# A graph layer on one core: 102 tiles of gathered rows handed from GpSimd's queue to column copies and single-row transfers

## The reference

```python
h = jnp.maximum(_layernorm(x, axis=-1), 0.0)
h_edge = ((h[src] + edge_attr_64) @ W).reshape(-1, H, D)
el = jnp.einsum('ehd,hd->eh', h_edge, attn_l)
er = jnp.einsum('nhd,hd->nh', (h @ W).reshape(-1, H, D), attn_r)
s = el + er[dst]
s = jnp.where(s > 0, s, NEG_SLOPE * s)
ex = jnp.exp(s - jax.ops.segment_max(s, dst, num_segments=N)[dst])
alpha = ex / jax.ops.segment_sum(ex, dst, num_segments=N)[dst]
ft = jax.ops.segment_sum(h_edge * alpha[..., None], dst, num_segments=N)
g = ft.mean(axis=1)
g = (g - g.mean(axis=0)) / jnp.sqrt(g.var(axis=0) + BN_EPS) * bn_gamma + bn_beta
return x + jax.nn.relu(g)
```

## Time and profile before

| | |
|---|---|
| median of 3 runs | 2339.57 us (2338.94 to 2344.23) |
| span of the profiled execution | 2008.4 us |
| the profiled execution's own time | not given in the profile; the median is 331.2 us over the span |
| busy | PE 926.1 us (46%), DVE 1131.0 (56%), ACT 114.1 (6%), POOL 1485.0 (74%) |
| DMA | 157.09 MB, mean 78 GB/s |

### The profile page before, as it was taken

The page is one execution under the profiler, slowest core; times in us unless marked ns, Lnnn a source line. Parts: engine busy times, 40 slices in busy tenths (PEclk is TensorE's granted clock), DMA queues, the critical chain, the costliest instruction groups (busy, mean ns, idle before and its releaser), DMA issues.

```text
span 2008.4 us, 19568 instructions
## 1 busy us (share of the span) xinstructions
PE 926.1 (46%) x6252; PEld 662.6 (33%) x6252; DVE 1131.0 (56%) x3243; ACT 114.1 (6%) x239; POOL 1485.0 (74%) x1579
## 2 busy tenths in 40 slices
PE   3537545434443454344435543544355335534455
PEld 2425333323332332233323322332233223322245
DVE  7878656545554555455545554555455546554565
ACT  3410000000000000000000000000000000000002
POOL 7777777777777777777777777777777777777771
PEclk9758767666776676667766666666666666666676
DMA  8734322322232223222322232223222322232234
GB/s 232 182 70 124 92 59 60 81 70 60 60 85 66 60 60 91 60 59 60 92 60 59 60 92 59 59 60 92 59 60 60 91 60 60 60 91 60 60 69 133
DMA packets 73591, 157.09 MB, mean 78 GB/s; under 512 B 29092, under 2 KB 33712, under 8 KB 66832
## 3 DMA queue, kind: packets, MB, share of 16 engines
q0 software_dynamic: 50208, 53.02, 15.7%
q1 hardware_dynamic: 22162, 99.02, 14.9%
q10 hardware_dynamic: 1112, 3.73, 0.7%
HBM read 144.42 MB, written 9.80 MB: 77 GB/s over the span
## 4 chain that ended last, share of the span: by engine, by line
POOL 67%; issue 22%; DVE 4%; PE 3%; DMA 2%; ACT 0%; ACTq 0%; DVEq 0%; SPq 0%; POOLq 0%
POOL work L696 67%; PE p_s L944 1%; DMA er_run<-er_tab,er_idx 1%; DMA h_tab<-acc 1%; DMA acc<-in_x 1%; PE po L1082 1%; PE pt L933 0%; POOL er_run L710 0%; DVE acc L1261 0%; DVE acc L1259 0%; DVE acc L1569 0%; DVE work L1253 0%; DVE scaled L1251 0%; PE pt L1142 0%; DVE ohT_i L1363 0%
## 5 line engine op out<-in xcount | busy, mean ns | idle before, releaser
L696 POOL DMA_INDIRECT work<-h_tab,srcI x1498 | 1414.0, 944 | 456.5 <-issue 456.2
L1209 DVE COPY elh<-work 128x16 f32<-128x16 f32 x196 | 39.0, 199 | 731.9 <-DMA work<-h_tab,srcI 729.1
L1019 PE MATMUL p_s<-ident,elh 128*32 128x128 f32 x196 | 50.6, 411 | 769.6 <-DVE elh L1209 769.6
L1082 PE MATMUL po<-scaled,work 128*65 128x64 f32 x3104 | 250.0, 257 | 77.8 <-issue 74.8
L1019 PEld LDWEIGHTS p_s<-ident,elh 128*32 128x32 f32 x196 | 25.7, 155 | 780.9 <-DVE elh L1209 777.0
L1082 PEld LDWEIGHTS po<-scaled,work 128*65 128x65 f32 x3104 | 244.6, 173 | 88.1 <-issue 87.2
L982 PE MATMUL p_s<-work,wpair 128*32 128x256 f32 x784 | 235.8, 468 | 15.6 <-DVE p_r L1487 14.0
L969 PE MATMUL pt<-ident,work 128*128 128x128 f32 x784 | 158.2, 353 | 60.6 <-DVE work L1214 59.8
L1569 DVE TENSOR_TENSOR acc<-acc,po 65x64 f32 x776 | 168.3, 217 | 28.8 <-DVE acc L1569 2.7
L969 PEld LDWEIGHTS pt<-ident,work 128*128 128x128 f32 x784 | 124.1, 183 | 89.4 <-DVE work L1214 84.6
L982 PEld LDWEIGHTS p_s<-work,wpair 128*32 128x32 f32 x784 | 100.6, 134 | 146.0 <-issue 68.1
(11 more groups left out here) (212 smaller groups left out, 945.6 us busy)
## 6 DMA issues: line engine op xcount, KB each, us to landing
work<-in_ea_t SPq DMA_DIRECT2D x49, 1024.0 KB, 6.4
ohT_i<-in_dst_n SPq DMA_DIRECT2D x49, 512.0 KB, 3.4
work<-h_tab,srcI POOLq DMA_INDIRECT x1498, 2.5
acc<-hT_tab SPq DMA_DIRECT2D x2, 1562.5 KB, 14.4
h_tab<-acc SPq DMA_DIRECT2D x1, 2887.5 KB
work<-in_x SPq DMA_DIRECT2D x1, 2800.0 KB
out<-work SPq DMA_DIRECT2D x5, 448.0 KB
acc<-in_x ACTq DMA_DIRECT2D x3, 672.0 KB
```

What stands on the lines that cost most here:

```text
L696: pool.indirect_dma_start(out=row, out_offset=None, in_=x if c < RAW else h_tab, in_offset=bass.IndirectOffsetOnAxis(ap=srcI[:, c, j, g:g ...
L1019: m = mm(sT_ps[:, j * P:(j + 1) * P], elh[:, c % 2, j, :, :].rearrange("p h g -> p (h g)"), ident[:, :], start=False, stop=True, skip_grou ...
L1082: m = mm(bank[0:F1, w0:w0 + H * WIN], edge[c % 2][:, j, g, :], scaled[:, j * CG + g, :, :].rearrange("p h w -> p (h w)"), start=(j == 0), ...
```

## The change

Two constants. COL_FIRST goes from NCH = 49 to 5: every chunk from 5 on gets column tiles at group 12, both halves, or only half 0 in chunks with c % 4 = 1 and in the last; that is 11 x 1 + 1 + 32 x 2 = 76 tiles. ROW_FIRST goes from NCH - 1 = 48 to 6: from chunk 6 to 47 five chunks of eight get a row tile at half 1 of group 15, 26 tiles, beside the one of the last chunk. tiles_of leaves these 102 tiles out of POOL's gathers. ScalarE gets 261 batches of 32 column copies and VectorE 43; SP gets 208 batches of 16 single-row transfers more.

```diff
-ROW_FIRST = NCH - 1
+ROW_FIRST = 6
 BATCH = 16
 BATCHES = (3, 2)
 ROW_SPAN, ROW_SHARE = 8, 5
 COL_G = 12
-COL_FIRST = NCH
+COL_FIRST = 5
 COL_BUFS = 4
 COL_BATCH = 32
 COL_BATCHES = (6, 1)
```

## The result

| | median, us | lowest to highest | runs |
|---|---|---|---|
| before | 2340.32 | 2338.94 to 2344.23 | 4 |
| changed | 3053.81 | 3036.99 to 3057.94 | 4 |

The ratio is 1.3032, 95% interval 1.2988 to 1.3075: 713 us slower, where 127 us faster was forecast.

A forecast was written before the change was run, and what follows sets the result against it. POOL's gathers, one every 1.2486 us, were taken to bound the kernel; 102 fewer save 127.4 us, with other engines' added work hidden and 331.2 us outside the span unchanged: 2339.6 - 127.4 = 2212 us, range 2185 to 2295.

The forecast's parts named there:

- the first one: Whole run: profiled span 2008.4 us against median 2339.57; the 331.2 us outside the span are carried unchanged.
- Rival 2: Time outside the span shrinks with the gathers (factor 1.165): saving 148 us, 2191 us; chance 0.12.
- POOL's part: POOL's gathers in the main loop: 102 fewer at 1.2486 us save 127.4 us; a full chunk takes 37.0 us.
- ScalarE's copy: Pitch of ScalarE's column copies with their address instructions: 0.107 us, with ends 0.09 and 0.203.
- ScalarE will come a little late to its exps: Head of ScalarE's chunk: exp's wait for VectorE makes its chunk 37.4 us, covered by 9 us of room.
- SP's part: SP's queue: five batches of 16 row transfers at 6.66 us plus 1.6 for bulk loads, 34.9 us a chunk.
- Hidden, by 2.6 us: Destinations queued behind SP's rows land at 36.7 us; VectorE's make_near asks for them at 39.3.
- rival 4: SP sets the pace: 0.05 us more a row makes 38.9 us a chunk, 2292 us in all; chance 0.07.
- VectorE: VectorE's one column batch a chunk, after the first eight adds: 5.3 us, upper end 8.5, hidden in waits.
- Rival 6: VectorE's copies each stop POOL for 0.14 us, 4.5 us a chunk: 2406 us; chance 0.04.
- Rival 5: ScalarE's copies don't overlap or pay for address instructions (0.153 to 0.203 us): 2534 to 2957 us; chance 0.06.
- Costed at nothing: Added VectorE and TensorE work (3 us a chunk of matmuls under 17.85 idle) was taken to add no time.

The follow-up runs named there:

- rows alone: Kernel before with only ROW_FIRST changed (26 more row tiles, no column tiles): 1977.08 us, ratio 0.9840, in ordinary surroundings; 2751.76 us, ratio 1.1842, in slow ones.
- the kernel with idle copies and rows: Kernel before plus unused ScalarE copies, SP row transfers and small DMA pieces in some chunks: 2008.95 us in ordinary surroundings; 2444.60 us, ratio 1.0456, in slow ones.

## Why the prediction was wrong

The forecast failed, and with it the direction. By its own steps:

- **The failed step is the first one**: "331.2 us lie outside what a trace can explain. I make the sum against the span and carry the 331.2 us unchanged". They lie inside. Spans in slow surroundings are as much longer as the times, and they consist of POOL waiting. A difference of 16% between a profile and the median was not a remainder to carry but the sign that profile and runs were made in different surroundings. With it fell the two terms that were to fit under POOL's 37.0 us: ScalarE's 35.5 us a chunk are 63.2 in the chunk shown (62 in the mean of the main loop), SP's 33.3 for five batches are 58.8, and POOL stands 25.5 us of each chunk for them. Rival 2 took the same difference as a factor on the gathers' pitch, with the opposite sign of what it did.
- **POOL's part** (127.4 us, 1.2486 a gather, a chunk of 37.0): right in ordinary surroundings (125.7 us; 37.35 in the chunk shown; "issue" as only releaser). In slow surroundings the gathers keep their pitch and saving them is worth nothing, since POOL then waits the longer.
- **ScalarE's copy** (0.107 us, from 0.203 less 0.096 at the clears' seams): right to the digit, 3.51 us for 32. The register load was 1.97, not 2.3, so its chunk is 6 x 5.47 + 1.2 = 34.0, not 35.5. "ScalarE will come a little late to its exps": in 44 of the 49 chunks it still waits for VectorE before them, 132.0 us in all, 3.0 each.
- **SP's part** (33.3 us for five batches): 32.0 from the first row to the last, with four of the five loads inside; right with the fifth. In slow surroundings it is 53.7 with rows alone and 58.8 in the result. "Hidden, by 2.6 us" failed there: VectorE waited 337.0 us over 38 chunks for the destinations, and rival 4 (SP sets the pace, 0.07, upper end 38.9 us) had this place and a small fraction of the size.
- **VectorE** (5.3 us for its batch, upper end 8.5): 2.38 for the load and 4.30 for the copies, 6.7 us. Hidden, as costed, in ordinary surroundings.
- **Rival 6**, gathers stopped by VectorE's copies: not seen. 1396 gathers beside 1376 such copies have a median of 947 ns and none is over 1.064 us in ordinary surroundings. The Trainium skill, SBUF — State Buffer, section SBUF: two separate sides, would have made of them stalls of POOL; these copies of 32 x 2 values don't show it, and in the slow surroundings, too, POOL's gathers stay at 948 ns while it is the others that crawl.
- **Rival 5** had the right place ("at the exp at the head of each chunk, behind which p_turned and with it POOL's gather 17 stand") and the wrong reason and chance (0.06). Its copies were to fail to overlap, at 0.153 to 0.203 us. What they took on average in the chunk shown is (63.2 - 6 x 1.97 - 1.2) / 192 = 0.26 us, beyond my upper end: a mixture of 0.107 and of crawls at 0.7 and 1.40.
- **"Costed at nothing"** rested on covers of waiting time. A cover in time is not enough where the queue that issues the work crawls. In 2168 us of the result's trace (from 400.3 to 2568.1) POOL's stretches of gathers are 1271 us long, and in them ScalarE starts 2518 copies, one in 0.50 us; the other 4180 start in the 896 us in which POOL stands, one in 0.21. So a chunk's gathers let some 72 of a chunk's 192 copies pass, and POOL stands still for the others.

**What stays open:** why the surroundings differ. The same kernel shows both, the same chip showed both in different groups, and within a group all runs agree. Not tried was any kernel that takes the gathers themselves away in the slow surroundings, so that it is gathers (and not another work of POOL) that slow the queues is what the rows suggest, and not shown by a run of its own. Nor is it shown whether TensorE's late signals and the crawl have one cause.

One rival stands that no run here tests: the recording itself. The runs made for this study, the timed ones too, each have a span and a granted clock, so each was recorded while it was timed. In the slow surroundings the records have gaps. Of the changed kernel, the trace from ordinary surroundings holds 38031 updates of semaphores and that of the result 13446; of the kernel with idle copies and rows it is 35414 and 8932. The records of instructions are as many in both. If writing these records is what lags there, the crawl is a cost of being recorded, and a run without a profile might not show it.

## What to carry to other kernels

Hold the span of a profile against the timed runs before using either: where they differ by more than a few us, the profile was made under other conditions, and costs read from it hold for those alone. Moving work from one engine's long instructions to hundreds of short ones on others saves time only as long as those are issued freely; count instructions per queue, not only busy time, and ask what the plan becomes if each costs several times as much. A kernel with idle work in some of its chunks carries its own comparison, and prices an instruction even when the surroundings can't be chosen.

## What the runs showed of the hardware

- In the slow surroundings instructions of ScalarE, VectorE, TensorE and SP start in steps of about 0.70 us in the later part of each stretch of GpSimd's gathers, and for some 2 us after it. The first of a stretch are quick: in the kernel with idle work TensorE still ran 64 matmuls in 6.34 us from 2.2 us after the first gather. Outside the crawl, a pair of address instruction and copy takes 0.107 us. The gathers keep their 1.25 us.
- There, too, the update of TensorE's semaphore came 10.6 us after its matmul in the chunks without idle work, against 0.01 us in ordinary surroundings.
- 2048 DMA pieces of 8 bytes more a chunk cost nothing there: 45.8 us a chunk with and without.
- An ACT copy of 32x2 values with a register address: 0.201 us, pitch 0.107; on VectorE pitch 0.134. A load of 32 registers: 1.97 us on ScalarE, 2.38 on VectorE; of 16 on SP 1.23.
- TensorE's granted clock was 0.632 of full speed in the result's trace, 0.705 in that of the same kernel in ordinary surroundings, means over stretches at its two levels, 1.2 and 2.4 GHz; TensorE was busy 41% of the one and 57% of the other. No run separates what that took from the crawling queues; both would end in POOL's waits.
